# An attention block whose probability-times-value product runs in blocks of four steps instead of two

## The reference, cut to what matters

```
mod = (silu(c) @ wmod).reshape(16, 6, 1, 256)          # sa, ca, ga, sb, cb, gb
h = layernorm(x) * (1 + ca) + sa
q = (h @ Wq.T) ; kv = h @ Wkv_down.T                    # 8 heads of 64; kv has 64 columns
k = kv @ Wk_up.T ; v = kv @ Wv_up.T
attn = softmax(q @ k.T / 8, axis=-1)                    # per batch and head, 1024 x 1024
x = x + ga * ((attn @ v) @ Wo.T)
h = layernorm(x) * (1 + cb) + sb
x = x + gb * (h @ weight.T + pooled(h) @ disha)         # pooled: sums over four groups of 64 features
```

## Time and profile before

| what | us |
|---|---|
| runs: lowest, median, highest | 3256.48, 3259.14, 3263.53 |
| the profiled execution | 3262.56 |
| its span, first to last instruction | 3260.8 |
| TensorE products busy in the span | 3175.0 (97%) |
| GpSimd busy | 2584.8 (79%) |
| VectorE busy | 2200.4 (67%) |
| ScalarE busy | 1705.1 (52%) |
| mean granted TensorE clock | 0.981 |

### The profile page before, as it was taken

One profiled execution on the slowest core, in us unless ns is written; L12 is line 12 of the kernel. 1 busy time (PEld: TensorE's weight loads), 2 busy tenths in 40 slices (PEclk: granted clock), 3 DMA queues, 4 the chain that ended last, 5 costly groups with the idle time before them and its releaser, 6 DMA issues.

```text
span 3260.8 us, 44881 instructions
## 1 busy us (share of the span) xinstructions
PE 3175.0 (97%) x15398; PEld 1927.1 (59%) x15398; DVE 2200.4 (67%) x2542; ACT 1705.1 (52%) x3203; POOL 2584.8 (79%) x1513
## 2 busy tenths in 40 slices
PE   5999999999999999999999999999999999999995
PEld 3555656566566665665666565665656656666554
DVE  4657676776767767677776767767677776766652
ACT  1555555555555555555555555555555555555451
POOL 1778788887888878788887878878788887877882
PEclk7999999999999999999999999999999999999995
DMA  2111111111112011121111112111110111111111
GB/s 68 40 44 55 46 66 33 49 60 47 56 47 66 31 58 53 47 66 33 53 56 47 56 47 66 35 55 52 47 66 34 53 56 46 56 46 53 43 34 36
DMA packets 161746, 163.16 MB, mean 50 GB/s; under 512 B 58480, under 2 KB 109808, under 8 KB 161520
## 3 DMA queue, kind: packets, MB, share of 16 engines
q1 hardware_dynamic: 161520, 160.30, 15.0%
HBM read 74.66 MB, written 17.33 MB: 28 GB/s over the span
## 4 chain that ended last, share of the span: by engine, by line
PE 92%; DVE 5%; POOL 1%; issue 1%; ACT 1%; DMA 1%; SPq 0%; POOLq 0%; ACTq 0%; DVEq 0%
PE ps_mix L547 27%; PE ps_score L565 16%; PE ps_max L586 14%; PE ps_score L567 14%; PE ps_side L535 6%; PE ps_side L646 6%; PE ps_side L664 3%; PE ps_side L633 2%; DVE neg_max L984 1%; DVE w_out_lo L993 1%; POOL prob_sum L842 1%; PE ps_side L604 1%; DVE query L1027 1%; PE ps_side L653 1%; DVE h_lo L1017 1%
## 5 line engine op out<-in xcount | busy, mean ns | idle before, releaser
L842 POOL TENSOR_TENSOR prob_sum<-prob_sum,probs 128x1024 f32<-128x1024 f32 x768 | 1881.0, 2449 | 243.4 <-ACT probs L722 188.2
L984 DVE TENSOR_REDUCE neg_max<-ps_max 128x1 f32<-128x1024 f32 x1024 | 1247.9, 1220 | 755.3 <-PE ps_max L586 749.3
L722 ACT ACTIVATE probs<-ps_score 128x512 f32<-128x512 f32 x2048 | 1113.3, 598 | 969.0 <-PE ps_score L567 956.5
L547 PE MATMUL ps_mix<-probs,values 128*64 128x512 f32 x4096 | 991.6, 605 | 0.0
L565 PE MATMUL ps_score<-query,key_hi 128*128 128x512 f32 x2048 | 873.7, 427 | 1.1 <-ACT probs L722 1.1
L567 PE MATMUL ps_score<-query_m,key_lo 128*128 128x512 f32 x2048 | 805.0, 393 | 0.0
L586 PE MATMUL ps_max<-key_hi,query 128*128 128x512 f32 x2048 | 644.5, 396 | 8.3 <-DVE neg_max L984 5.4
L565 PEld LDWEIGHTS ps_score<-query,key_hi 128*128 128x128 f32 x2048 | 384.6, 188 | 326.7 <-issue 246.2
L547 PEld LDWEIGHTS ps_mix<-probs,values 128*64 128x64 f32 x4096 | 248.4, 136 | 477.8 <-issue 477.1
L842 POOL TENSOR_TENSOR prob_sum<-probs 128x1024 f32<-128x1024 f32 x128 | 328.9, 2570 | 228.6 <-ACT probs L722 228.3
L586 PEld LDWEIGHTS ps_max<-key_hi,query 128*128 128x128 f32 x2048 | 386.2, 189 | 102.3 <-DVE neg_max L984 10.9
(11 more groups left out here) (119 smaller groups left out, 2907.5 us busy)
## 6 DMA issues: line engine op xcount, KB each, us to landing
query_m<-query SPq DMA_DIRECT2D x128, 512.0 KB, 3.2
recip<-recip_scratch SPq DMA_DIRECT2D x256, 128.0 KB, 2.9
x_in<-in_L_attn_x_dram SPq DMA_DIRECT2D x32, 512.0 KB, 4.0
x_mid<-in_L_attn_x_dram SPq DMA_DIRECT2D x64, 256.0 KB, 4.5
out_dram<-x_mid SPq DMA_DIRECT2D x64, 256.0 KB, 2.2
denoms<-recip SPq DMA_DIRECT2D x512, 1.0 KB, 1.7
gates<-gates_scratch SPq DMA_DIRECT2D x16, 256.0 KB, 4.1
query_m<-max_row SPq DMA_DIRECT2D x128, 4.0 KB
```

What stands on the lines that cost most here:

```text
L547: last = nc.tensor.matmul(ps_mix[j * R:j * R + R, :], values[par][:, k, :], probs[:, s % RING, j * HALF:(j + 1) * HALF], start=(k == 0), s ...
L722: nc.scalar.activation(probs[:, s % RING, half * HALF:(half + 1) * HALF], ps_score[half], ACT.Exp, scale=SCALE).then_inc(exps_done, 1)
L842: nc.gpsimd.tensor_tensor(out=total[:, :], in0=before, in1=probs[:, s % RING, :], op=ALU.add).then_inc(adds_done, 1)
L984: nc.vector.tensor_reduce(neg_max[:, m:m + 1], ps_max[m % 2][:, :], AX_X, ALU.max, negate=True).then_inc(maxima_done, 1)
```

## The change

The mix runs in blocks of four steps, in steps 1, 5, 9 and so on, so the ring of probabilities gets six steps. The room for it comes from `mixed`: two buffers of four pairs become one of eleven half-rows that two batches share, one of them in reverse order, with a wait on `mixed_split` before an overwritten half-row. The table of steps moves: turned maxima go from step 1 of a group to step 5, denominators from step 3 to step 1 of the next group (as counted from the group's own start, from 11 to 9), and the normalisations on GpSimd, two transposes, splits and output projections go a few steps up or down. The multiplication stands four steps behind the denominators, not five.

```diff
-RING = 4
+RING = 6
-SPREAD_LAG, RECIP_LAG, OUT_LAG, BACK_LAG, MIX_LAG = 1, 2, 2, 3, 5
-MIXED = 2
+SPREAD_LAG, RECIP_LAG, OUT_LAG, BACK_LAG, MIX_LAG = 1, 2, 2, 3, 4
+MIXED = 4
-OUT_GATES_LOAD, OUT_GATE, OUT_HI, OUT_LO = 44, 52, 54, (56, 59)
-FFN_GATE, FFN_HI, FFN_LO = (1, 8), (3, 9), (7, 11)
+OUT_GATES_LOAD, OUT_GATE, OUT_HI, OUT_LO = 44, 52, 54, (57, 61)
+FFN_GATE, FFN_HI, FFN_LO = (1, 2), (3, 3), (7, 5)
     "query": (40, 42, 50, 58, STEPS, STEPS + 2, STEPS + 4, STEPS + 6),
-    "norm_t": (8, 10, 16, 18),
+    "norm_t": (8, 12, 16, 20),
     "latent": (26, 32),
     "values_t": (54, 60),
-    "mixed_hi": (9, 16, 24, 40),
+    "mixed_hi": (6, 15, 24, 40),
-    "norm2": (16, 25, 38, 49),
+    "norm2": (18, 26, 38, 50),
     "norm2_t": (24, 34, 48, 56),
...
-        "max_row": STEPS - NT + 1 + NT * i,
-        "denominator": NT * (i + 1) + 3,
+        "max_row": STEPS - NT + 5 + NT * i,
+        "denominator": NT * (i + 1) + 1,
...
-        mixed = [sb(f"mixed{i}", [P, PAIRS, T]) for i in range(2)]
+        mixed = sb("mixed", [P, 2 * PAIRS + 3, HALF])
...
+        def mixed_block(par, p, half):
+            base, count = (0, PAIRS + 1) if half == 0 else (PAIRS + 1, PAIRS + 2)
+            return mixed[:, base + (count - 1 - p if par else p), :]
...
-                                     probs[:, s % RING, j * HALF:(j + 1) * HALF],
+                                     probs[:, (STEPS * z.c + s) % RING, j * HALF:(j + 1) * HALF],
...
+                        if zg.has_o and p > half:
+                            need(act, mixed_split, CHUNKS * zg.o + 2 * (half + 1))
```

More of the change, by code:

```diff
@@ L272, in adaln_block @@
         w_ffn_gated = x_norm2[:, :, :]
-        stage = [m[:, :, :].rearrange("p a t -> p (a t)") for m in mixed]
+        stage = [probs[:, 2:, :].rearrange("p a t -> p (a t)"), mixed[:, :, :].rearrange("p a t -> p (a t)")]
         s_wmod = stage[0][:, 0:3072].rearrange("p (k n) -> p k n", k=NF)
@@ L296, in mixed_parts, with mixed_chunk @@
             return mixed_hi[:, :, :], mixed_lo[:, :, :]
+        def mixed_block(par, p, half):
+            base, count = (0, PAIRS + 1) if half == 0 else (PAIRS + 1, PAIRS + 2)
+            return mixed[:, base + (count - 1 - p if par else p), :]
+        def mixed_chunk(par, g):
+            base, count = (0, PAIRS + 1) if g < CHUNKS // 2 else (PAIRS + 1, PAIRS + 2)
+            at = base + (count - PAIRS if par else 0)
+            return mixed[:, at:at + PAIRS, (g % 2) * CT * P:(g % 2 + 1) * CT * P]
         def group_queries(g):
@@ L645, in side_work @@
                         for q, (mp, wp, p) in enumerate(products):
+                            pair = PAIRS - 1 - p if (1 - z.par) else p
                             last = nc.tensor.matmul(side[:, 0:D], mp[:, p, j * P:(j + 1) * P],
-                                                    wp[:, p, :], start=(q == 0), stop=(q == len(products) - 1))
+                                                    wp[:, pair, :], start=(q == 0), stop=(q == len(products) - 1))
                     elif kind == "norm2_t":
@@ L721, in slot @@
                             need(act, scores_ready, 2 * (STEPS * z.c + s) + half + 1)
-                            nc.scalar.activation(probs[:, s % RING, half * HALF:(half + 1) * HALF], ps_score[half],
+                            nc.scalar.activation(probs[:, (STEPS * z.c + s) % RING, half * HALF:(half + 1) * HALF], ps_score[half],
                                                  ACT.Exp, scale=SCALE).then_inc(exps_done, 1)
@@ L728, in slot @@
                         need(act, group_done, GROUPS * zg.c + g + 1)
-                        nc.scalar.activation(mixed[zg.par][:, p, half * HALF:(half + 1) * HALF], ps_mix[:, :],
+                        if zg.has_o and p > half:
+                            need(act, mixed_split, CHUNKS * zg.o + 2 * (half + 1))
+                        nc.scalar.activation(mixed_block(zg.par, p, half), ps_mix[:, :],
                                              ACT.Copy).then_inc(group_evacuated, 1)
@@ L840, in add_probs @@
                     need(pool, adds_done, done)
-                before = probs[:, (s - 1) % RING, :] if k == 1 else total[:, :]
-                nc.gpsimd.tensor_tensor(out=total[:, :], in0=before, in1=probs[:, s % RING, :], op=ALU.add).then_inc(adds_done, 1)
+                now = STEPS * z.c + s
+                before = probs[:, (now - 1) % RING, :] if k == 1 else total[:, :]
+                nc.gpsimd.tensor_tensor(out=total[:, :], in0=before, in1=probs[:, now % RING, :], op=ALU.add).then_inc(adds_done, 1)
             def slot(z):
@@ L970, in divide @@
                         p, half = divmod(i, 2)
-                        raw = mixed[mpar][:, p, half * HALF:(half + 1) * HALF]
+                        raw = mixed_block(mpar, p, half)
                         nc.vector.tensor_tensor(raw, raw, recip[:, :], ALU.mult).then_inc(group_mixed, 1)
@@ L998, in slot @@
                             hi, lo = mixed_parts(z, g)
-                            nc.vector.tensor_tensor(lo, mixed[1 - z.par][:, :, g * CT * P:(g + 1) * CT * P],
+                            nc.vector.tensor_tensor(lo, mixed_chunk(1 - z.par, g),
                                                     hi.bitcast(F32), ALU.subtract).then_inc(mixed_split, 1)
```

8 lines of the change are left out of this document (4 added, 4 removed).

## The result

The changed kernel takes 3319.7 us (median of four runs, 3315.7 to 3327.1), the kernel before on the same chip 3261.3: a ratio of 1.018, 95% interval 1.016 to 1.021. The direction was forecast, the size was not: 58 us more instead of 23. The profiled execution has a span of 3313.9 us, 53.1 more than before.

A forecast was written before the change was run, and what follows sets the result against it. The prediction took TensorE, which hardly rests, as the bound: 3262.6 - 87 (fewer blocks) + 104 (steps without cover) - 5 (waits gone) + 11 (GpSimd) = 3285.6, less 3.4 for the median, so 3282 us, 0.7% slower; range 3240 to 3318.

The forecast's parts named there:

- blocks: Mix blocks on TensorE: 255 fewer, each saving 0.34 us for entering, leaving and a fixed part inside; 87 us gained.
- queries ahead of bare steps: Steps with scores and maxima alone, behind a query ScalarE must clear: 77 places at 0.82 us, 63 us lost.
- latent, transposes, values: Steps with scores and maxima alone behind these pieces: 0.56, 0.62 and 0.45 us in 15 batches, 24 us lost.
- other bare steps, mixed_hi, last batch: Other steps with scores and maxima alone, 14 us; late exponentials at step 16, 1.5; last batch without maxima, 1.5.
- waits that go: TensorE's wait at denominators for a query VectorE has not cleared disappears: 5 us gained.
- GpSimd at step 57: Denominators moved from step 59 to 57 wait 0.8 us for GpSimd's addition in 14 batches: 11 us lost.
- start and tail: Program's start and end: no change, plus or minus 2 us.
- The rival in which only the drain is saved: Fewer mix blocks save only entering and leaving, 49 us, not the 0.15 inside each: 3320 us; chance 7%.
- The price of bare steps: Steps with scores and maxima alone make TensorE wait for ScalarE's exponentials: 104 us lost in all.
- the rule that the weight load stands behind the wait: After scores-and-maxima-only steps, weights load only once exponentials' first half ends; second product starts 0.98 us after exponentials start.
- The rival in which weights are loaded during the wait: Weights are ready when exponentials end, so the price is 76 us: 3254 us, not slower; chance 24%.
- The rival with GpSimd 2 us later at several denominators: GpSimd's additions take longer beside VectorE; denominators of 57, perhaps 9, wait 2 us more: 3307 us; chance 14%.

The follow-up runs named there:

- Experiment 5: The changed kernel with pieces exchanged, those ScalarE clears one step ahead of a block, those VectorE clears ahead of a step without one: 3280.0 us, 1.0041.
- experiment 2: The changed kernel with GpSimd's additions of probabilities cut to the first 8 of 1024 columns: 3272.8 us, 1.0027 to the kernel before.
- experiment 1: The changed kernel with the normalising multiplication six steps behind its denominators instead of four, first mixed_hi at step 8: 3291.9 us, 1.0085 to the kernel before.
- experiment 3: The changed kernel with GpSimd's last normalisation at step 49 instead of 50: 3314.5 us, 1.0157 to the kernel before.

## Why the prediction was right on the sign and wrong on the size

Terms of the sum, for the profiled executions (us):

| term | forecast | measured | from |
|---|---|---|---|
| blocks | -87 | -87 | 0.34 a block, table of steps |
| queries ahead of bare steps | 63 | 64 | steps 43, 51, 59, 3, 7, each less 1.392 |
| latent, transposes, values | 24 | 26 | steps 27, 35, 55 |
| other bare steps, mixed_hi, last batch | 17 | 17 | eight steps a batch, 0.14 each |
| first score after a bare step | in the above | 3 | 2.83 for 2.79 at five steps |
| waits that go | -5 | about -5 | step 59 loses the wait of the earlier trace rows |
| GpSimd at step 57 | 11 | 16.5 | 1.0 in 13 batches, 3.0 in the first |
| VectorE late | 0 | 27 | 7.8 at step 8; 19 at 16, 17, 24, 25 |
| start and tail | 0 | -8 | 3.0 more, 11.4 less |
| sum | 23 | 53 | |

- **The gain** was right, down to the 0.15 inside a block. The rival in which only the drain is saved named 3320 us, and the runs took 3319.7; that is chance, since the step lengths show 0.34 a block and not 0.19. The Trainium skill, "TensorEngine Tiling (Array Packing)", Key Properties, names a drain when the tiling mode changes. The trace agrees as far as entering and leaving go; these two alone would have given 49 us of the 87.
- **The price of bare steps** was right, 110 for 104, and with it the rule that the weight load stands behind the wait. The rival in which weights are loaded during the wait fell: in step 51 the load itself waits 0.98 for the exponentials. Experiment 5 shows that the price behind a query is ScalarE's. The turned maxima, charged at nothing, cost nothing: TensorE waits for their row once in the whole program, 0.3 us.
- **The step that failed** is this sentence: "Normalisations, w_ffn_lo, mixed_lo and w_out_lo on VectorE now lie in block steps of 5 us, which hide them; without that cover VectorE's reductions would hold the maxima." The block hides one of them, not two, once each lasts up to 3.0 us and the first starts only when the DMA has landed; and in step 8 the late VectorE held not only the maxima but the clearing of a query. These are the groups of VectorE's instructions in the kernel before, to be held against those under experiment 2:

```profile
L972 DVE TENSOR_TENSOR mixed<-mixed,recip 128x512 f32<-128x512 f32 x128 | 95.8, 748 | 13.1 <-DMA recip<-recip_scratch 12.9
L988 DVE TENSOR_TENSOR w_ffn_lo<-x_norm,w_ffn_hi 128x512 fp32r<-128x512 f32 x16 | 26.9, 1679 | 0.0
```

There the multiplication took 0.75 us on average, 125 of 128 under 1.0, and waited 13 us in all for the DMA. At its new place 75 of 128 take over 1.0, since GpSimd is adding there, the mean is 1.53, and the waits come to 224 us. The forecast looked at where the work lies, and not at how long it takes beside its new neighbours, nor at how long it waits there with other work behind it. I had the late maxima among the things that would prove me wrong, but not in the sum and not as a rival. The term is worth 27 us in the trace, 28 by experiment 1.
- **GpSimd** was the right place and 0.2 a batch too small (1.0 for 0.8; its work from the addition of step 51 on took 0.3 longer than I carried over), and the first batch, where the steps are shorter, waits 3.0. The rival with GpSimd 2 us later at several denominators fell: the others don't wait. The reason for the early part of the lateness, which experiment 3 tested, was wrong.
- **Start and tail** differ mostly by the granted clock, and that they took 8 us off the sum is luck: over the twelve traces the tail lies between 71 and 82 us, and the kernel with the changed buffers alone, in the order of before, has 78. At the start the products that fold the weights took 0.63 us each instead of 0.38. After the last denominators TensorE waits 13 us in both kernels (13.6 and 13.2), and then the output products ran at different granted clocks. Windows of TensorE alone (stretch, length, busy, clock, DMA share, GB/s), before and after:

```profile
3204.00:3212.00 8.00, 6.78 (x30) 0.50 0.00 1
```

```profile
3268.00:3276.00 8.00, 4.42 (x33) 1.00 0.00 0
```

That is 1.2 against 2.4 GHz. Of the 11.4 us that the tail took less, 9.6 lie behind the start of these products; the other 1.8 lie ahead of it, where the last denominators waited 3.0 us for GpSimd before and 0.7 after. The median of the changed kernel lies 4 us above its profiled run; where the other runs lost them no trace shows.

## What to carry to other kernels

A piece taken away from an engine that never rests is worth its fixed cost only if what it hid is hidden by something else: list every wait that ended under it, put behind it what another engine needs time to clear, and give the bare places to pieces that the busy helper doesn't touch. When an operation is moved on an engine with an in-order queue, its duration has to be taken from rows in which the neighbours do what they will do at the new place, and its wait there counts for everything that stands behind it in the queue. A stretch in which an engine works without a gap is shortened only by taking work out of it, not by reordering what stands ahead of its last rest.

## What the hardware showed that was not expected

VectorE's operations on two SBUF operands (SBUF is the on-chip memory) last very differently here: 0.69 us for 128x512 when no addition of GpSimd is running, up to 3.0 when one of 2.4 us is; with the additions cut to 8 columns the means are 685 to 697 ns. Its reductions from PSUM take 1.2 us in all these runs. The Trainium skill, "SBUF — State Buffer", section "SBUF: two separate sides", says that the two engines share a pair of ports by an exclusive lock, which whoever starts first holds for its whole instruction. The trace agrees: 2.81 is 0.69 and most of an addition, and in batch 5, where the multiplication starts 0.06 us ahead of an addition, it takes its 0.69 and the addition 2.9 instead of 2.4. A small difference decides: between steps 21 and 24 the multiplication takes 0.69 in the seven batches in which it starts at most 4.38 us after the second score product of step 21, and 2.5 to 2.9 in the seven in which it starts 4.44 or more after. So the same step has two lengths in the same program, 1.82 or 3.07 at step 24, in seven batches each.

The first batch pays more for the late maxima, 8 of the 27 us: without the previous batch's pieces its steps are shorter. There TensorE stood 2.4 us at step 16, and the windows show the granted clock of that stretch at 0.79, the mean of its two levels over 8 us; in the kernel before it is 1.00 from 104 to 176 us:

```profile
136.00:144.00 8.00, 5.64 (x21) 0.79 0.17 66
```
